# A state-space layer whose batches' closing and opening share one step, on one Trainium2 core

## The chip, the core and the metric

The kernel runs on 1 core of one Trainium2 chip. The metric is device time in microseconds (us) for one execution, lower is better. The engines are named as in the profile: PE is the matmul engine, DVE the vector engine, ACT the scalar (activation) engine, POOL the GpSimd engine, SP the queue that issues transfers.

## What is computed

A decoder of four layers, twelve sublayers in all, on `x` of 4 batches of 1024 tokens, 256 features each, float32. Each sublayer is `x = layernorm(x + sublayer(x))`. The change touches one of the twelve, the state-space layer (`L2_attn`):

```python
def _L2_attn_ref(x, norm_w, in_proj_w, conv_w, conv_b, x_proj_w, dt_proj_w, dt_proj_b, A_log, D, out_proj_w):
    # inner width 512, 16 states, 4 taps, rank 64
    x_copy = x
    h = x * jax.lax.rsqrt(jnp.mean(x * x, axis=-1, keepdims=True) + 1e-05) * norm_w
    xs, res = jnp.split(h @ in_proj_w.T, 2, axis=-1)
    xc = conv_general_dilated(xs over the tokens, conv_w, 4 taps, causal, one filter per feature) + conv_b
    u = silu(xc)
    delta, Bm, Cm = jnp.split(u @ x_proj_w.T, [64, 80], axis=-1)
    delta = softplus(delta @ dt_proj_w.T + dt_proj_b)
    # for every token: state = exp(delta * -exp(A_log)) * state + delta * u * Bm ; y = sum_n state * Cm
    y = y + u * D
    y = y * silu(res)
    return y @ out_proj_w.T + x_copy
```

The layer returns `x_copy` too, so the sum that is normalised behind it is `2 * x + y @ out_proj_w.T`.

## The kernel before

The residual stream stays on the chip for the whole program, as `chip.xt` (128 partitions x 2 feature chunks x 4096 tokens), features on partitions. The program is a row of *steps*. A step is one block in which each engine has its own hand-written instruction list, with semaphores between them; it ends in `all_engine_barrier`, so no engine starts the next step before all have finished this one. The order within an engine is exactly as written; no scheduler moves anything.

`state_space` (L3120) loads the weights and then runs a hardware loop (`nc.Fori`, L3167) over the four batches. `halves` is 2: a batch's 1024 tokens are worked in two groups of 512. `SC` is 4: the inner width of 512 is four chunks of 128. `FC` is 2, the chunks of the 256 features. One turn of the loop is four steps:

- `ssm_inputs` (L3177), the **opening**. ACT squares x (L3197), PE sums the squares over the features with a matmul by constants (L3216), ACT takes the root (L3201), DVE the reciprocal (L3232) and the scaled input `ssm_in` (L3234), for one half and then the other: both halves use the same buffer `rms`, so the second root waits until the first half is scaled. Only when both halves are scaled does PE run the 16 input products (L3223, jobs `(m, j)`: chunk m, half j; 32 matmuls). ACT copies the first eight into `ssm_x` (L3207) and puts the last eight through Silu into `ssm_gate` (L3209).
- `ssm_steps` (L3239). DVE does the convolution, for each of four chunks one multiply-add with a scalar (L3269) and three with an accumulator (L3271), out of `ssm_x` into `ssm_pre`; ACT puts each chunk through Silu into `ssm_u` (L3323); PE multiplies with `x_w` and `states_w` (L3352, L3353) and ACT copies the sums out (L3325). The rest of the step makes the decays' exponents and the rows for the scan.
- `ssm_scan` (L3391), 64 scans of 1024 tokens (16 states x 4 chunks) on DVE, with PE, ACT and POOL around them. Its buffers are `decay`, `state` and `term`. Its last instruction is DVE's multiplication with the gate (L3494).
- `add_norm` (L98), the **closing**. PE multiplies with `out_w` (L138, 16 matmuls), DVE adds twice the residual (L184), ACT squares (L170), PE sums over the features into 4 columns for each half (L151, 1-column matmuls), ACT takes roots (L173), DVE reciprocals (L198), PE spreads them over the partitions (L157), DVE writes the normalised residual (L203).

A float32 matmul is two rows of the trace, called *passes* below: the 32 matmuls of L3223 are 64 rows. Of on-chip matmul memory (8 banks) the closing took all 8, and the opening 6.

## Time and profile before

| what | us |
| --- | --- |
| median of 3 runs | 10751.27 |
| lowest, highest run | 10743.31, 10764.56 |
| the profiled execution, its own time | 10734.41 |
| its span, from the first to the last instruction | 10731.0 |
| the state-space layer's loop in it (four batches) | 5741.61 to 7240.34 |

The profile is of one execution. Lines such as L3223 are lines of the program before. The mean granted clock of PE over the span is 0.855 of full speed (2.4 GHz). The state-space loop is 1499 us of the 10731, some 375 us for each batch; the other eleven sublayers are the rest, and the change leaves them alone.

### The profile page before, as it was taken

The numbers are of one execution on the slowest core, as the hardware profiler recorded it, in microseconds if no ns is written. First come the engines' busy times: TensorE is split into PE (matmuls) and PEld (weight loads), VectorE is DVE, ScalarE is ACT, GpSimd is POOL, SyncE is SP. The second block draws the span as 40 slices with busy tenths as digits, with TensorE's granted clock in tenths as the row PEclk, the third lists the DMA queues.
The fourth block names the chain that finished last, engine by engine and source line by source line (L and its number), as shares of the span: only waits on it lengthen the run. The fifth ranks groups of instructions, "written<-read, shape, count | busy, mean of one in ns | idle before, by whom it ended". The sixth has DMA issues, their size and how long they took to land. (4 is left out here: it accounts for less than half of the span.)

```text
span 10731.0 us, 120768 instructions
## 1 busy us (share of the span) xinstructions
PE 8366.6 (78%) x42322; PEld 4574.4 (43%) x42322; DVE 5866.2 (55%) x11337; ACT 4361.6 (41%) x7541; POOL 2286.8 (21%) x2066
## 2 busy tenths in 40 slices
PE   4877584975989889889896887888886899656565
PEld 1222253542333356546643444444343444345454
DVE  6777341025767556336525786684643656555554
ACT  3666230112555555326413674562221444333332
POOL 1110112021101011001100442350000100366666
PEclk8888676986999889989996988898887999778787
DMA  3221232112212100000000000000001332366656
GB/s 65 44 45 31 47 70 75 63 55 41 34 29 41 24 13 2 9 12 2 10 0 13 1 1 1 1 1 10 5 1 24 50 52 43 107 188 184 186 179 188
DMA packets 243500, 521.79 MB, mean 49 GB/s; under 512 B 55051, under 2 KB 94837, under 8 KB 241431
## 3 DMA queue, kind: packets, MB, share of 16 engines
q1 hardware_dynamic: 154887, 232.49, 10.9%
q0 software_dynamic: 88064, 282.15, 8.8%
q8 instruction: 324, 5.31, 0.2%
q14 instruction: 225, 1.84, 0.1%
HBM read 425.31 MB, written 75.53 MB: 47 GB/s over the span
## 5 line engine op out<-in xcount | busy, mean ns | idle before, releaser
L818 ACT ACTIVATE probs<-scores 128x1024 f32<-128x1024 f32 (+4 forms) x960 | 868.5, 937 | 889.5 <-PE scores L695 634.1
L907 DVE TENSOR_REDUCE row_max<-ring 128x1 f32<-128x512 f32 (+3 forms) x1792 | 1025.8, 627 | 246.3 <-PE ring L669 220.4
L695 PE MATMUL scores<-query_stack,key_stack 99*128 99x512 bf16 (+3 forms) x2816 | 851.2, 394 | 164.6 <-DVE levels L929 77.8
L3568 POOL DMA_INDIRECT r_got<-in_L_ffn_tables,r_pick_now x832 | 814.2, 979 | 329.6 <-issue 244.9
L3693 PE MATMUL r_psum_y<-r_diagonal,r_got 128*128 128x128 f32 x4096 | 582.2, 311 | 363.5 <-ACT r_diagonal L3750 363.5
L715 PE MATMUL outputs<-probs,head_values 128*32 128x512 f32 (+3 forms) x5632 | 780.4, 629 | 101.8 <-ACT probs L815 99.3
L3693 PEld LDWEIGHTS r_psum_y<-r_diagonal,r_got 128*128 128x128 f32 x4096 | 566.0, 225 | 424.7 <-ACT r_diagonal L3750 419.0
L815 ACT ACTIVATE probs<-levels,quant 128x1024 f32<-128x1024 uint8 x512 | 612.7, 1233 | 326.0 <-DVE levels L929 322.4
L929 DVE TENSOR_SCALAR levels<-scores 128x1024 uint8<-128x1024 f32 x512 | 607.6, 1220 | 179.9 <-PE scores L695 145.1
L669 PE MATMUL ring<-key_stack,query_stack 96*128 96x512 bf16 (+3 forms) x1792 | 608.2, 382 | 63.3 <-DMA key_stack<-normed_parts 39.5
L3502 DVE TENSOR_TENSOR_SCAN state<-decay,added 128x1024 f32<-128x1024 f32 x256 | 571.0, 2271 | 32.4 <-ACT decay L3460 32.4
L695 PEld LDWEIGHTS scores<-query_stack,key_stack 99*128 99x128 bf16 x2816 | 257.4, 104 | 689.1 <-DVE levels L929 279.9
L3437 PE MATMUL state_sums<-term,constants 128*128 128x512 f32 x1024 | 497.6, 609 | 42.7 <-POOL term L3468 34.0
L2994 POOL TENSOR_TENSOR norm_squares<-qk,rope 128x256 f32<-128x256 f32 x256 | 180.8, 740 | 1573.2 <-DVE qk L2918 1573.2
L3852 DVE CUSTOM_DVE_ANT_0 r_scratch<-r_got,r_rows_now 128x256 f32<-128x256 f32 x1024 | 374.3, 423 | 73.1 <-DMA r_got<-in_L_ffn_tables,r_pick_now 61.8
L2725 PE MATMUL window_products<-wide_w,shifted 128*128 128x512 f32 x768 | 365.2, 627 | 58.2 <-DVE shifted L2895 49.6
L3456 ACT ACTIVATE added_rows<-ssm_du_rows,ssm_state_in_rows 128x128 f32<-128x128 f32 x1280 | 398.3, 386 | 3.5 <-PEq L63 3.5
L669 PEld LDWEIGHTS ring<-key_stack,query_stack 96*128 96x128 bf16 x1792 | 171.3, 103 | 500.8 <-DVE row_max L907 302.8
L3049 PE MATMUL gated_psum<-norm_sum,gated_w 128*128 128x512 f32 x768 | 346.4, 614 | 6.8 <-DVE norm_sum L3096 6.8
L3460 ACT ACTIVATE decay<-ssm_dt,a_log 128x1024 f32<-128x1024 f32 x256 | 292.5, 1142 | 127.1 <-DVE state L3502 127.0
L3750 ACT ACTIVATE r_diagonal<-constants,r_act 128x128 f32<-128x128 f32 x1024 | 313.1, 388 | 57.9 <-DVE r_act L3857 57.4
L3428 PEld LDWEIGHTS added<-constants,added_rows 128*128 128x128 f32 x2048 | 246.6, 145 | 162.9 <-issue 135.4
(645 smaller groups left out, 15577.2 us busy)
## 6 DMA issues: line engine op xcount, KB each, us to landing
joined_heads<-heads_out SPq DMA_DIRECT2D x512, 32.0 KB, 2.0
expert_w<-in_L_ffn_w SPq DMA_DIRECT2D x16, 1024.0 KB, 10.9
r_got<-in_L_ffn_tables,r_pick_now POOLq DMA_INDIRECT x832, 3.7
quant_parts<-parts SPq DMA_DIRECT2D x48, 256.0 KB, 4.9
query_stack<-quant_parts SPq DMA_DIRECT2D x48, 256.0 KB, 8.5
key_stack<-quant_parts SPq DMA_DIRECT2D x48, 256.0 KB, 8.8
query_stack<-cross_parts SPq DMA_DIRECT2D x48, 256.0 KB, 8.3
normed_parts<-parts SPq DMA_DIRECT2D x48, 256.0 KB, 5.3
```

What stands on the lines that cost most here:

```text
L669: last = nc.tensor.matmul(out[:, 0:cols], lhs, k_stack[0:max_row, h, j * GROUP:j * GROUP + cols], start=True, stop=not edge)
L695: last = nc.tensor.matmul(out[:, off:GROUP], keys, q_stack[0:rows, h, half * GROUP + off:(half + 1) * GROUP], start=True, stop=not edge)
L715: last = nc.tensor.matmul(o_ps[SLOT * i:SLOT * (i + 1), half % out_banks, off:GROUP], vals, probs[0:k_rows, n % 2, i // 2, i % 2, off:GROU ...
L815: nc.scalar.activation(dst, levels[:, e % 2, :, :], ACT.Exp, bias=quant[:, 4:5], scale=scale).then_inc(probs_ready, 1)
L818: nc.scalar.activation(dst, s_ps[0:k_rows, 2 * (e % 2):2 * (e % 2) + 2, off:GROUP], ACT.Exp, scale=scale).then_inc(probs_ready, 1)
L907: nc.vector.reduce_max(row_max[:, i, qt, at:at + 1], src[:, 0:cols], AX.X).then_inc(ring_read, 1)
L929: ts(levels[:, e % 2, :, :], s_ps[:, 2 * (e % 2):2 * (e % 2) + 2, :], 0.0, QMAX, ALU.max, ALU.min).then_inc(scores_read, 1)
L3437: last = nc.tensor.matmul(sum_ps[:, half(j)], chip.c(C_ID), term[:, i % 2, half(j)], start=(n == 0), stop=(n == STATES - 1))
L3456: last = nc.scalar.activation(scaled[:, i % 2, t, :], du_rows[:, t, c, :], ACT.Copy, scale=b_rows[:, t, n:n + 1])
L3502: nc.vector.tensor_tensor_scan(state[:, i % 2, :], decay[:, i % 2, :], added[:, i % 2, :], 0.0, ALU.mult, ALU.add).then_inc(state_ready, 1)
L3568: nc.gpsimd.indirect_dma_start(out=b["got"][:, n, :], out_offset=None, in_=b["tables"], in_offset=bass.IndirectOffsetOnAxis(ap=b[picks][:, ...
L3693: last = nc.tensor.matmul(y_ps[:, c, t * P:(t + 1) * P], row, b["diagonal"][:, k % 2, n, :], start=False, stop=(k == RHEADS * per - 1 and ...
```

## The change

The loop's body is cut at another place. A new step `ssm_between(closing, opening)` holds a batch's closing together with the next batch's opening and its convolution. It is written out once with only the opening (batch 0), stands in the loop for batches 0 to 2 (closing b, opening b + 1), and is written out once more with only the closing (batch 3). What lies between, `ssm_steps` and `ssm_scan`, is in the loop body for three batches and is written out behind the loop for the fourth. Diff, cut:

```diff
-        with nc.Fori(0, BATCH) as b:
-            ssm_inputs(chip, b, w_in, norm_w, xs, gate)
-            ssm_steps(chip, conv, per_feature, w_x, w_states, w_dt, xs, states, u, dt, du_rows, b_rows, pick, kept)
-            ssm_scan(chip, a_log, pick, kept, states, u, dt, du_rows, b_rows, gate, per_feature)
-            with banks(nc, "norm_psum", [P, 8, GROUP], F32) as norm_ps:
-
-                add_norm(chip, [bass.ds(b * SEQ + j * GROUP, GROUP) for j in range(halves)], norm_ps, keeps=2.0, zero_mean=True,
-                         product=(w_out, lambda j, k: u[:, k, j * GROUP:(j + 1) * GROUP]))
...
+        pre = sb("ssm_pre", [P, SC, SEQ])
+
+        def middle():
+            ssm_steps(chip, pre, per_feature, w_x, w_states, w_dt, states, u, dt, du_rows, b_rows, pick, kept)
+            ssm_scan(chip, pre, a_log, pick, kept, states, u, dt, du_rows, b_rows, gate, per_feature)
+
+        between = lambda closing, opening: ssm_between(chip, closing, opening, w_in, norm_w, conv, per_feature, w_out, xs, gate, u, pre)
+        between(None, 0)
+        with nc.Fori(0, BATCH - 1) as b:
+            middle()
+            between(b, b + 1)
+        middle()
+        between(BATCH - 1, None)
...
+        sq_in = ctx.enter_context(sbuf(nc, "ssm_in_squares", [P, halves, FC, GROUP], F32))
+        rms = ctx.enter_context(sbuf(nc, "ssm_in_rms", [P, halves, GROUP], F32))
+        y_ps = ctx.enter_context(banks(nc, "ssm_out_psum", [P, halves, FC, GROUP], F32))
         in_ps = ctx.enter_context(banks(nc, "ssm_in_psum", [P, 4, GROUP], F32))
...
+        mean_ps = lambda j: in_ps[:, 2 + j, :]
+        rstd_ps = lambda g: y_ps[:, g, 0, :]
...
+                if opens:
+                    for j in range(halves):
+                        for c in range(FC):
+                            nc.scalar.activation(sq_in[:, j, c, :], x_in(c, j), ACT.Square).then_inc(in_squared, 1)
+                    for j in range(halves):
+                        act.wait_ge(in_mean, j + 1)
+                        nc.scalar.activation(rms[:, j, :], mean_ps(j), ACT.Sqrt, bias=chip.eps[:, 0:1]).then_inc(rms_ready, 1)
+                squares(0)
+                squares(1)
+                copied(0, 2)
+                deviation(0)
+                copied(2, 3)
+                deviation(1)
+                copied(3, len(jobs))
...
+                output(0, 0)
+                mean(0)
+                output(0, 1)
+                mean(1)
+                output(1, 0)
+                output(1, 1)
+                inputs(0, 2)
+                variance(0)
+                inputs(2, 3)
+                variance(1)
+                inputs(3, 5)
+                spread(0)
+                inputs(5, 6)
+                spread(1)
+                inputs(6, len(jobs))
...
+                add(0, 0)
+                scaled(0)
+                add(0, 1)
+                scaled(1)
+                add(1, 0)
+                add(1, 1)
+                inverse(0)
+                inverse(1)
+                convolve(0)
+                normalise(0)
+                normalise(1)
+                for c in range(1, SC):
+                    convolve(c)
...
@@ -3319,7 +3414,6 @@
             @block.scalar
             def _(act):
                 for c in range(SC):
-                    act.wait_ge(conv_ready, c + 1)
                     nc.scalar.activation(u[:, c, :], pre[:, c, :], ACT.Silu).then_inc(u_ready, 1)
...
-        decay, state, term = (sb(n, [P, 2, SEQ]) for n in ("decay", "state", "term"))
+        decay, state = spare[:, 0:2, :], spare[:, 2:4, :]
+        term = sb("term", [P, 2, SEQ])
```

`spare` is `pre`. In the new step `output` is the product with `out_w`, `mean` the sum of x's squares, `inputs` the input products, `variance` and `spread` the closing's small matmuls, `add`, `inverse` and `normalise` its work on DVE, `scaled` the reciprocal and the two multiplications of the opening. PE waits for `h_ready` half by half (`j + 1`), where it waited for both. ACT's dummy root ahead of the closing (L164) is gone. In both built programs `decay`, `state` and `term` lie at the same bytes of a partition (from 185184, 193376 and 201568), since `ssm_pre` was the first buffer of the step before the scan and gave its place to `decay` and `state` when that step ended.

PE before: the opening, at the head of the loop's body, and the closing, at its end; between the last row and the next batch's first stand a barrier and the loop's branch:

```order
L3211 UNCONDITIONAL_BRANCH
L3216 MATMUL ssm_mean<-norm_squares,constants 128x512 x4
L3223 MATMUL ssm_in_psum<-ssm_in,in_w 128x512 x32
...
L130 UNCONDITIONAL_BRANCH
L138 MATMUL norm_psum<-ssm_u,out_w 128x512 x16
L151 MATMUL norm_psum<-constants,norm_squares 128x1 x16
L157 MATMUL norm_psum<-constants,norm_root 128x128 x8
```

Nothing of the one can run beside the other there.

PE after, the merged step in the loop, from its start:

```order
L3251 MATMUL ssm_out_psum<-ssm_u,out_w 128x512 x4
L3245 MATMUL ssm_in_psum<-ssm_in_squares,constants 128x512 x2
L3251 MATMUL ssm_out_psum<-ssm_u,out_w 128x512 x4
L3245 MATMUL ssm_in_psum<-ssm_in_squares,constants 128x512 x2
L3251 MATMUL ssm_out_psum<-ssm_u,out_w 128x512 x8
L3276 MATMUL ssm_in_psum<-ssm_in,in_w 128x512 x4
L3259 MATMUL ssm_out_psum<-constants,norm_squares 128x1 x8
L3276 MATMUL ssm_in_psum<-ssm_in,in_w 128x512 x2
L3259 MATMUL ssm_out_psum<-constants,norm_squares 128x1 x8
L3276 MATMUL ssm_in_psum<-ssm_in,in_w 128x512 x4
L3266 MATMUL ssm_out_psum<-constants,norm_root 128x128 x4
L3276 MATMUL ssm_in_psum<-ssm_in,in_w 128x512 x2
```

The same 76 matmuls stand in one row now, the opening's sums of squares under the closing's products, and the closing's small matmuls between the first input products; four more of L3266 and twenty of L3276 follow.

DVE after, the middle of the merged step, behind the scaled inputs (before, the convolution L3269 and L3271 stood at the head of the next step, and the residual's L203 at the end of the closing):

```order
L3303 SCALAR_TENSOR_TENSOR norm_sum<-residual,ssm_out_psum 128x512
L3303 ISA
L3303 SCALAR_TENSOR_TENSOR norm_sum<-residual,ssm_out_psum 128x512
L3316 RECIPROCAL norm_root<-norm_root 128x4 x2
L3328 TENSOR_SCALAR ssm_pre<-ssm_x,conv_w,ssm_vectors 128x1024
L3330 SCALAR_TENSOR_TENSOR ssm_pre<-ssm_x,conv_w,ssm_pre 128x1024 x3
L3322 TENSOR_TENSOR residual<-norm_sum,ssm_out_psum 128x512 x4
```

The first chunk's convolution now stands between the closing's reciprocals and its last four instructions; the other three chunks follow behind them, in the same step as PE's input products.

## Rows read from the trace of the kernel before

**Rows 1.** Stretches: us; busy us per engine (instructions); PE's granted clock; DMA share; GB/s.

```profile
core 0: us, PE busy (x) PEld busy (x) DVE busy (x) ACT busy (x) POOL busy (x), PEclk, DMA share, GB/s
5740.54:5814.59 74.05, 55.25 (x104) 18.95 (x104) 27.94 (x23) 21.20 (x30) 0.00 (x0) 0.83 0.00 0
6089.04:6190.03 100.99, 76.49 (x184) 31.23 (x184) 33.53 (x32) 25.73 (x37) 0.00 (x0) 0.84 0.00 1
6190.03:6463.98 273.95, 233.56 (x960) 135.52 (x960) 235.10 (x140) 194.56 (x414) 138.80 (x102) 0.87 0.00 1
6463.98:6565.33 101.35, 77.65 (x184) 31.43 (x184) 33.53 (x32) 25.73 (x37) 0.00 (x0) 0.84 0.00 1
6838.79:6943.88 105.09, 79.89 (x184) 33.99 (x184) 33.61 (x33) 25.72 (x37) 0.00 (x0) 0.79 0.00 1
7216.40:7240.34 23.94, 21.44 (x80) 12.69 (x80) 5.67 (x11) 4.53 (x8) 0.00 (x0) 0.87 0.00 1
```

**Rows 2.** Timeline, batch 0's closing: start us, us, engine, line, idle before and its releaser.

```profile
6087.81 1.23 DVE L3494 TENSOR_TENSOR ssm_u<-ssm_u,ssm_gate 128x1024 f32<-128x1024 f32 x1
...
6090.53 15.75 PE L138 MATMUL norm_psum<-ssm_u,out_w 128*128 128x512 f32 x32 [4.07 <-PEq L63]
...
6096.14 0.69 DVE L184 SCALAR_TENSOR_TENSOR norm_sum<-residual,norm_psum 128x512 f32<-128x512 f32 x1 [7.10 <-PE norm_psum L138]
...
6106.12 3.66 PE L151 MATMUL norm_psum<-constants,norm_squares 128*128 128x1 f32 x32
...
6109.65 2.03 PE L157 MATMUL norm_psum<-constants,norm_root 128*128 128x128 f32 x16
...
6110.82 2.48 DVE L203 TENSOR_TENSOR residual<-norm_sum,norm_psum 128x512 f32 x4 [0.52 <-PE norm_psum L157]
```

**Rows 3.** Timeline, batch 1's opening.

```profile
6116.99 1.28 ACT L3197 ACT_TABLE_LOAD   x1 [6.91 <-issue]
...
6119.49 3.78 PE L3216 MATMUL ssm_mean<-norm_squares,constants 128*128 128x512 f32 x4 [7.81 <-ACT norm_squares L3197]
...
6124.03 3.35 DVE L3232 RECIPROCAL norm_sum<-norm_sum 128x512 f32<-128x512 f32 x1 [10.72 <-ACT norm_sum L3201]
...
6125.08 3.54 PE L3216 MATMUL ssm_mean<-norm_squares,constants 128*128 128x512 f32 x4 [1.81 <-ACT norm_squares L3197]
...
6129.77 3.35 DVE L3232 RECIPROCAL norm_sum<-norm_sum 128x512 f32<-128x512 f32 x1 [0.82 <-ACT norm_sum L3201]
...
6134.73 29.59 PE L3223 MATMUL ssm_in_psum<-ssm_in,in_w 128*128 128x512 f32 x64 [6.11 <-DVE ssm_in L3234]
...
6162.64 0.60 ACT L3209 ACTIVATE ssm_gate<-ssm_in_psum 128x512 f32<-128x512 f32 x1 [1.12 <-PE ssm_in_psum L3223]
...
6164.35 0.60 ACT L3209 ACTIVATE ssm_gate<-ssm_in_psum 128x512 f32<-128x512 f32 x1 [1.12 <-PE ssm_in_psum L3223]
```

**Rows 4.** Timeline, head of the step behind it.

```profile
6165.63 0.81 DVE L3269 TENSOR_SCALAR ssm_pre<-ssm_x,conv_w,ssm_vectors 128x1024 f32<-128x1024 f32 x1 [30.96 <-PEq L63]
6166.48 3.93 DVE L3271 SCALAR_TENSOR_TENSOR ssm_pre<-ssm_x,conv_w,ssm_pre 128x1024 f32<-128x1024 f32 x3
...
6170.44 1.06 ACT L3323 ACTIVATE ssm_u<-ssm_pre 128x1024 f32<-128x1024 f32 x1 [5.49 <-DVE ssm_pre L3271]
...
6171.55 1.97 PE L3352 MATMUL ssm_low_psum<-ssm_u,x_w 128*64 128x512 f32 x2 [7.23 <-ACT ssm_u L3323]
...
6190.03 1.02 ACT L3325 ACTIVATE ssm_low<-ssm_low_psum 64x1024 f32<-64x1024 f32 x1 [4.47 <-PE ssm_states_psum L3353]
```

**Rows 5.** Stretches, small closing matmuls of batches 0 and 2; columns as in Rows 1.

```profile
6106.00:6112.00 6.00, 5.68 (x49) 5.36 (x47) 2.23 (x5) 1.16 (x3) 0.00 (x0) 1.00 0.01 3
6856.00:6866.00 10.00, 8.60 (x50) 8.06 (x48) 3.61 (x7) 1.16 (x3) 0.00 (x0) 0.64 0.01 2
```

**Rows 6.** Timeline, entry into the loop, first batch.

```profile
5739.02 1.52 DVE L237 TENSOR_SCALAR out_w<-out_w,weight_means 128x256 f32<-128x256 f32 x4
5741.61 1.28 ACT L3197 ACT_TABLE_LOAD   x1 [8.97 <-PEq L63]
```

More of the change, by code:

```diff
@@ new lines, in ssm_between @@
+        jobs = [(m, j) for m in range(2 * SC) for j in range(halves)]
+        half = lambda j: slice(j * GROUP, (j + 1) * GROUP)
+        x_in = lambda c, j: chip.xt[:, c, bass.ds(opening * SEQ + j * GROUP, GROUP)]
+        x_out = lambda c, g: chip.xt[:, c, bass.ds(closing * SEQ + g * GROUP, GROUP)]
+        with step(nc, "in_squared in_mean rms_ready h_ready in_ready in_copied y_ready summed squared var_ready root_ready inverse_ready rstd_ready dve_step") as (
+                block, in_squared, in_mean, rms_ready, h_ready, in_ready, in_copied, y_ready, summed, squared, var_ready, root_ready, inverse_ready, rstd_ready, dve_step):
@@ new lines, in squares, with deviation @@
+                def squares(g):
+                    for c in range(FC if closes else 0):
+                        act.wait_ge(summed, FC * g + c + 1)
+                        nc.scalar.activation(sq[:, g, c, :], z[:, g, c, :], ACT.Square).then_inc(squared, 1)
+                def deviation(g):
+                    if closes:
+                        act.wait_ge(var_ready, g + 1)
+                        nc.scalar.activation(root[:, g, :], rstd_ps(g)[:, 0:per], ACT.Sqrt, bias=chip.eps[:, 0:1]).then_inc(root_ready, 1)
@@ new lines, in spread, with inputs @@
+                def spread(g):
+                    if closes:
+                        pe.wait_ge(inverse_ready, g + 1)
+                        for t in range(per):
+                            last = nc.tensor.matmul(rstd_ps(g)[:, t * P:(t + 1) * P], root[:, g, t:t + 1].to_broadcast((P, P)), chip.c(C_ID), start=True, stop=True)
+                        last.then_inc(rstd_ready, 1)
+                def inputs(first, end):
+                    for n in range(first, end if opens else first):
+                        m, j = jobs[n]
+                        pe.wait_ge(h_ready, j + 1)
+                        if n >= 4:
+                            pe.wait_ge(in_copied, n - 3)
+                        for c in range(FC):
+                            last = nc.tensor.matmul(in_ps[:, n % 4, :], w_in[:, c, m * P:(m + 1) * P], h[:, c, half(j)], start=(c == 0), stop=(c == FC - 1))
+                        last.then_inc(in_ready, 1)
@@ L3388, with ssm_scan @@
 TURNED_BY_POOL = 3
[L3391 removed]
+def ssm_scan(chip, spare, a, pick, kept, states, u, dt, du_rows, b_rows, gate, per_feature):
     nc = chip.nc
```

123 lines of the change are left out of this document (62 added, 61 removed).

## The prediction

> **What bounds the kernel now.** I read the page's list of engines and its costliest lines first, then the table of stretches around the state-space layer, then the timeline there. The other eleven sublayers don't change, so only this layer's loop matters. A batch of it falls into a middle and a boundary. The middle (from the copy L3325 to the gate L3494) takes 273.95 us with DVE busy 235 [rows 1]; its instructions are the same before and after, and the scan's buffers lie at the same bytes, so I let it stand. The boundary, from the end of L3494 to the next batch's copy L3325, takes 100.99, 101.35 and 105.09 us at the three places, 307.4 in all. DVE is busy for 33.5 us of each and ACT for 25.7, PE for 76.5, and with its clock at 0.84 [rows 1]. So no engine fills a boundary: it is a chain of steps in which one engine works and the others wait at a barrier.
>
> The pieces of the first boundary, by the timeline: 1.49 us from the gate's end (6087.81 + 1.23) to PE's first product [rows 2]; closing 22.77, to the end of L203 at 6113.30 [rows 2]; 3.69 of barrier and loop branch to ACT's table load at 6116.99 [rows 2, 3]; opening 47.96, to the end of the last Silu at 6164.95 [rows 3]; 0.68 of barrier; 5.92 for the first chunk's convolution and Silu, until PE starts at 6171.55; 18.48 for the products with x_w and states_w, until the copy at 6190.03 [rows 4]. Sum 100.99.
>
> Inside the opening PE stands still while ACT and DVE make the scaled input: from 6119.49, its first mean, to 6134.73 it does 7.3 us of work in 15.2, and the last stretch is two reciprocals of 3.35 us one behind the other [rows 3]. In the closing PE is never idle for more than a handoff, but DVE and ACT are. That is what a merge can use.
>
> **The merged step.** PE's list is what sets its length if nothing in it waits. The closing's 32 passes take 15.75 us, with a slow start in it [rows 2]. The four means, 8 passes, ran at a low clock, 3.78 and 3.54 us [rows 3]; under the products they are in a warm stretch, where four passes take 1.71 us (the distance of the last two Silus, 6162.64 and 6164.35 [rows 3]), so 3.4. The input products are 64 passes, 16 jobs x 1.71 = 27.4 (29.59 before, with a slow start [rows 3]). The small matmuls are 3.66 and 2.03 [rows 2]. Sum 52.3, and 0.6 for the last Silu: 52.9.
>
> Does anything in it wait? I lay the lists against each other, from PE's start as 0. ACT squares x from 0 to 2.3 (two take 1.15, the 1.15 to 1.2 between ACT's table load and PE's first mean [rows 3]), before PE's first mean at 5.5. Roots, reciprocal and scaling take 5.7 us for a half, from PE's mean (6119.49 + 3.78) to 6128.95 [rows 3]; the first half is scaled at 13.0, and the second, with one add before it on DVE, at 18.6. PE gets to the input products at 19.3, so they don't wait, by 0.7 us. Squares of the sums are ready at 20.9, and PE's second small group comes at 26.3. The two small roots come back at 25 and 28.6, their spreads stand at 31.5 and 34.2. DVE is free for the convolution at 28.9. A chunk takes 4.7 us (0.81 + 3.93 [rows 4]), the four residuals 2.5 [rows 2]: 28.9 + 18.8 + 2.5, and half a microsecond for a wait on the second spread, makes 50.7. That is 2.2 us before PE and ACT are done. So the convolution is hidden, with 2.2 us to spare; each microsecond more on DVE beyond that would lengthen the step by one.
>
> Closing and opening together go from 22.77 + 47.96 = 70.73 to 52.9: **17.8** less. One barrier goes, **0.7** [rows 3, 4]. The next step starts with a Silu of 1.06 us instead of 5.92 until PE starts, 1.1 with the handoff: **4.8** less [rows 4]. Behind it the 18.48 stays: PE's 32 passes there are back to back whether the other chunks come early or not (the fourth Silu was ready when PE got to it). One boundary gains 23.3, three gain **69.9**.
>
> **The loop's branch.** The loop turns three times instead of four, and the third boundary has no branch back. A turn costs 3.69 [rows 2, 3]; entering the loop costs 1.07, from the end of L237 (5740.54) to ACT's load [rows 6]. I take the difference, **2.6**, once. What the trace shows is that the way back costs more than the way in. The Trainium skill, "Runtime: NRT & Kernel Launch", section "Instruction fetch mechanics", says why this can be: a taken branch to code that isn't held makes the engine fetch it first, while straight code is streamed ahead. By that rule the copy of the middle behind the loop, which no taken branch back leads to, costs nothing and the sum is the one below; if new code cost as much as a turn, the sum would be 2.6 less.
>
> The copy of the middle is code that the trace of before does not show. Its bounds from rows are nothing and one turn's extra, 2.6. I take nothing, since the first batch entered code that had not run before at 1.07 [rows 6].
>
> **First opening and last closing.** The first stretch takes 74.05 [rows 1]. After, ACT needs no table load in front of its squares (the order has none there; 1.28 [rows 6]), and the second half's means and root don't wait for the first half's scaling. Means start at 1.2, the first half is scaled 9.46 later, the second 4.96 after that [rows 3], at 15.6; then 60 passes at 0.43 (25.8) and a slow start of 1.7, the last Silu: 43.7 against 47.9. That is 4.2, and 4.8 for the convolution, less 0.4 for entering the loop there: **8.6**. The last closing, 23.94 [rows 1], loses its early table load: the roots' load now stands behind the squares, 1.28 at most, mostly under PE's small matmuls. I take **-0.3**; bounds 0 and -1.28.
>
> **Clock.** The third boundary was 4.1 us longer than the first: in its small matmuls the granted clock was 0.64 against 1.00 [rows 5]. I leave one such spell in. It may go (4.1 more gain) or come at all three (8.2 less). PE's start after the merged step comes after 5.4 us of idling (0.6 + 3.7 + 1.1) instead of 7.23, so I leave its slow start in; its price is four passes at 3.78 instead of 1.71, 2.1 [rows 3]. The trace shows a slow start after 4.07 us of idling too [rows 2]. The Trainium skill, "TensorE: Matmul & The Clock Gate", Part 1, says that an array that has idled is granted half the pulses, and all after sustained work; rows 2, 3 and 5 fit that, and by it the merged step, with no idling in it, would keep the high level of 2.4 GHz.
>
> **Sum.** 69.9 + 2.6 + 8.6 - 0.3 = 80.8. The profiled execution took 10734.4 (its span 10731.0), so its like would take 10653.6. The median is 16.9 above it, so I subtract from the median, 10751.3: **10670.5**, 0.75% less.
>
> **Rivals.**
> - *More is gained*: PE stays at the high clock over the shorter gaps in all four steps behind an opening (4 x 2.1) and the slow spell goes (4.1): 10658. For it: the gap is shorter, at the copied middle only some 2.7 us. Against: 4.07 us were enough to go slow. 15%.
> - *The merged step stretches*: PE's waits for h_ready are only 0.7 us clear and DVE's end 2.2; with the slow level in the small matmuls and the products behind them in every boundary, 6 us each, 18 in all: 10689. For it: rows 5. Against: PE has 512-column work on both sides of each small group. 17%.
> - *It doesn't do what it says*, because the moved work was hidden before: about 10748. Against it: DVE waited 30.96 us in front of the convolution [rows 4] and PE 6.11 in front of the products [rows 3]. 4%.
> - *Slower*: PE runs the merged step at the low level, 1.2 GHz, throughout. A pass of 512 columns takes 0.43 at the high level (1.71 / 4 [rows 3]) and twice that at the low one; its 104 passes (32 + 8 + 64) would take 44.7 us more, and from some 63 slow passes in each boundary the 80.8 are gone, at 104 the time is 10671 + 3 x 44.7 = 10805. For it: nothing but that the step mixes tiny matmuls in, and rows 5. Against: the products with out_w and in_w came up to speed after at most some six passes each. 4%.
>
> **How the numbers follow.** Forecast 60%: around 10671, with 8 us of scatter between runs (lowest to median of the three shown) on either side, the spell's 4.1 and 8.2 and the closing's 1. To hold 8 in 10 the range takes in the first two rivals: down to 10658 less 10, up to 10689 plus 11: 10648 to 10700. 0.2%, 21.5 us, is about what a measurement of this kernel can tell from no change. Faster by more: 60 + 15 + 17 = 92%; same 4%; slower 4%.
>
> **What would show it.** The boundary in the loop: 77.7 us instead of 101, of which the merged step is 53 from PE's first product to the last Silu; PE without idle time in it; DVE's last convolution ended 2 us before the last Silu; the next step's first Silu at its very start. The third boundary some 2.6 shorter than the first two. The middle unchanged at 274. It is wrong if PE waits at the first input product, if DVE ends last, if the granted clock in the step is under 0.9, or if the middle after the loop is longer than those in it.

## The result, and the profile after

The changed kernel took 10649.2 us (median of four runs, 10625.6 to 10659.0), the kernel before in the same comparison 10750.3 (four runs, 10743.3 to 10764.6). The ratio is 0.9904, 95% interval 0.9889 to 0.9919: faster by 1.0%, where 0.75% was forecast; 0.9904 of 10751.3 is 10648, at the very edge of the range, 22 us below the forecast. The profiled run took 10658.0, its span 10656.2.

The first view is again the table of stretches: the opening (from the end of L237 to the first L3419, which was L3325 before), the three boundaries (end of the gate, now L3589, to the next L3419) and the last closing. The rows that answer to them are [rows 1]. Columns: stretch, us, busy us per engine (instructions), PE's granted clock, DMA share, GB/s.

```profile
core 0: us, PE busy (x) PEld busy (x) DVE busy (x) ACT busy (x) POOL busy (x), PEclk, DMA share, GB/s
5752.48:5816.42 63.94, 53.65 (x104) 18.57 (x104) 28.12 (x22) 19.58 (x28) 0.00 (x0) 0.88 0.00 0
6091.53:6170.72 79.19, 72.15 (x184) 30.04 (x184) 33.41 (x32) 22.45 (x35) 0.00 (x0) 0.91 0.00 1
6443.25:6519.56 76.31, 69.84 (x184) 29.46 (x184) 33.42 (x33) 22.44 (x34) 0.00 (x0) 0.93 0.00 1
6794.28:6868.06 73.78, 69.86 (x184) 29.45 (x184) 33.41 (x33) 22.44 (x34) 0.00 (x0) 0.95 0.00 1
...
7139.60:7163.40 23.80, 21.39 (x80) 12.66 (x80) 5.68 (x10) 4.33 (x7) 0.00 (x0) 0.87 0.00 1
```

PE has the same 184 passes in a boundary, in 74 to 79 us instead of 101 to 105. It is busy for 91 to 95% of a boundary, where it was for 76%. DVE's 33.4 us are as before, ACT's 22.4 are 3.3 fewer, mostly two table loads of 1.28: the work is the same, the waiting is gone.

The second view is the timeline of the merged step that closes batch 1 and opens batch 2, in order of time (start us, us, engine, line, operation, and in brackets the idle time before it with its releaser; one row can hold several instructions, as x8 says):

```profile
6442.03 1.22 DVE L3589 TENSOR_TENSOR ssm_u<-ssm_u,ssm_gate 128x1024 f32<-128x1024 f32 x1
...
6444.40 5.10 PE L3251 MATMUL ssm_out_psum<-ssm_u,out_w 128*128 128x512 f32 x8 [3.72 <-PEq L63]
...
6449.33 1.88 PE L3245 MATMUL ssm_in_psum<-ssm_in_squares,constants 128*128 128x512 f32 x4
...
6455.48 1.41 DVE L3310 SCALAR_TENSOR_TENSOR ssm_in<-residual,ssm_norm,ssm_in_rms 128x512 f32<-128x512 f32 x2 [0.16 <-DVE ssm_in_rms L3308]
...
6456.20 7.03 PE L3251 MATMUL ssm_out_psum<-ssm_u,out_w 128*128 128x512 f32 x16
...
6460.90 1.42 DVE L3310 SCALAR_TENSOR_TENSOR ssm_in<-residual,ssm_norm,ssm_in_rms 128x512 f32<-128x512 f32 x2
...
6463.07 3.60 PE L3276 MATMUL ssm_in_psum<-ssm_in,in_w 128*128 128x512 f32 x8
...
6466.50 1.84 PE L3259 MATMUL ssm_out_psum<-constants,norm_squares 128*128 128x1 f32 x16
...
6478.72 17.33 PE L3276 MATMUL ssm_in_psum<-ssm_in,in_w 128*128 128x512 f32 x40
```

No row of PE behind the first carries an idle time, through out_w's products, the sums of squares, the input products and the small groups: PE works from 6444.40 on without a wait. The second half of the scaled input is there at 6462.32 (6460.90 + 1.42), 0.75 us before the first input product at 6463.07. That product doesn't need it: its job is of the first half, and PE waits half by half. The first half was scaled at 6456.89 (6455.48 + 1.41), and the first job that needs the second half starts four passes later, at 6464.78. So the waits were clear by 6.2 and 2.5 us.

The end of that step and the head of the next, from the timelines of ACT, DVE and PE:

```profile
6496.10 0.60 ACT L3212 ACTIVATE ssm_gate<-ssm_in_psum 128x512 f32<-128x512 f32 x1 [1.12 <-PE ssm_in_psum L3276]
6500.24 3.89 ACT L3417 ACTIVATE ssm_u<-ssm_pre 128x1024 f32<-128x1024 f32 x4 [3.55 <-issue]
...
6490.60 3.92 DVE L3330 SCALAR_TENSOR_TENSOR ssm_pre<-ssm_x,conv_w,ssm_pre 128x1024 f32<-128x1024 f32 x3
...
6501.35 1.97 PE L3446 MATMUL ssm_low_psum<-ssm_u,x_w 128*64 128x512 f32 x2 [5.29 <-ACT ssm_u L3417]
```

DVE's last convolution ends at 6494.52, 2.18 us before the last Silu's end at 6496.70. Then ACT stands still for 3.55 us while the loop turns, and PE for 5.29. In front of the middle behind the loop the same two rows read:

```profile
6848.98 3.89 ACT L3417 ACTIVATE ssm_u<-ssm_pre 128x1024 f32<-128x1024 f32 x4 [1.02 <-PEq L63]
...
6850.09 1.97 PE L3446 MATMUL ssm_low_psum<-ssm_u,x_w 128*64 128x512 f32 x2 [2.76 <-ACT ssm_u L3417]
```

1.02 us against 3.55: the difference, 2.5, is what the loop's way back costs ACT.

Cut into the pieces of the prediction, in us (from PE's first product to the last Silu's end is the merged step):

| | forecast, in the loop / behind it | boundary 0 | boundary 1 | boundary 2 |
|---|---|---|---|---|
| gate's end to PE's first product | 1.49 | 1.41 | 1.15 | 1.12 |
| merged step | 52.9 | 53.94 | 52.30 | 52.57 |
| last Silu's end to PE's next product | 4.8 / 2.2 | 4.94 | 4.65 | 2.12 |
| until L3419 | 18.48 | 18.90 | 18.21 | 17.97 |
| sum | 77.7 / 75.1 | 79.19 | 76.31 | 73.78 |

The merged step took 53.94 us in boundary 0 and 52.3 to 52.6 in the others. The difference lies at its start, where PE runs out_w's products behind an idle time of 3.7 to 4 us: the granted clock of the first 8 us was 0.61 in boundary 0 and 0.82 in boundary 1. The last closing shows the same in two traces of the changed kernel. It took 23.8 us in this one, with 0.83 over its first 10 us, and 27.0 in the repeat below, with 0.66. The rows are the starts of boundary 0 and 1 and then the closings of this trace and of the repeat:

```profile
6092.94:6100.94 8.00, 8.00 (x12) 3.43 (x13) 0.69 (x1) 3.47 (x5) 0.00 (x0) 0.61 0.00 1
6444.40:6452.40 8.00, 8.00 (x16) 3.58 (x17) 1.12 (x2) 4.16 (x6) 0.00 (x0) 0.82 0.00 0
...
7139.60:7149.60 10.00, 8.95 (x18) 4.09 (x19) 1.03 (x2) 0.63 (x1) 0.00 (x0) 0.83 0.01 2
...
7153.99:7163.99 10.00, 8.91 (x14) 3.85 (x15) 0.69 (x1) 0.63 (x1) 0.00 (x0) 0.66 0.01 2
```

Such a slow start comes and goes between traces of one kernel, and is worth 1.6 us in a merged step and 3.2 in the last closing.

The whole layer, from the end of L237 to the residual's last write, took 1499.8 us before (5740.5 to 7240.3) and 1410.9 after (5752.5 to 7163.4): 88.9 less, of which the boundaries 78.2, the opening 10.1, the last closing 0.1 and the middles 0.5. The spans of the two profiled runs differ by 74.8 only: the layer began 11.9 us later in the run of the changed kernel, behind instructions that are the same in both, and what follows it took 2.2 us longer. The medians differ by 101 us, and the ratio makes it 103. The traced execution of before took 16 us less than its kernel's median, that of after 9 us more, so the two traces can't place the 12 to 14 us that the medians have beyond the layer's 89. The comparison was repeated below for this reason.

### The profile page after: what moved, and what is told of

Its sections match the earlier page's. It is cut to its first block and busy times, and to the rows that moved or that the text cites. A ratio compares the mean times of both kernels' runs of the same rounds, so it can differ in the third digit from the quotient of the medians.

```text
span 10656.2 us, 120727 instructions
## 1 busy us (share of the span) xinstructions
PE 8354.1 (78%) x42322; PEld 4572.8 (43%) x42322; DVE 5866.7 (55%) x11337; ACT 4348.3 (41%) x7530; POOL 2286.5 (21%) x2066
## 5 line engine op out<-in xcount | busy, mean ns | idle before, releaser
L3597 DVE TENSOR_TENSOR_SCAN ssm_pre<-ssm_pre,added 128x1024 f32<-128x1024 f32 x256 | 570.9, 2271 | 32.3 <-ACT ssm_pre L3555 32.3
L3555 ACT ACTIVATE ssm_pre<-ssm_dt,a_log 128x1024 f32<-128x1024 f32 x256 | 292.4, 1142 | 127.0 <-DVE ssm_pre L3597 127.0
```

The costliest lines, as they stand in the source:

```text
L3597: nc.vector.tensor_tensor_scan(state[:, i % 2, :], decay[:, i % 2, :], added[:, i % 2, :], 0.0, ALU.mult, ALU.add).then_inc(state_ready, 1)
```

## Experiments

The theory after the result: all of the gain that the change makes is in the four openings and closings of this layer, by the sum of the prediction with terms mis-sized; what differs from boundary to boundary is the loop's branch and PE's clock at the start of a step. The rivals: that one of the two halves of the change does all of it; that the branch is not what makes the third boundary shorter, or that a straight copy costs as much; that DVE's slack decides; that the extra 14 us of the first comparison are real. The layer's times below are taken from each kernel's trace between the same two instructions, since a layer can be read to some microseconds there, while a comparison of whole runs has an interval of about 20 us.

The kernel before took about 10970 us in all later comparisons, 220 more than in the first, but its layer was the same (1499.8 and 1499.1, below). Ratios, and the layer's microseconds, can be compared over these; times can't. The traces show where the 220 lie: the last sublayer, which fetches rows of tables by POOL's transfers, took 1505.7 and 1504.5 us in the traces of before and after, and 1698.6 to 1731.1 in the eleven later ones. Between 9320 and 10600 us the DMA engines moved 186 GB/s in the trace of before and 161 in that of `before_again`. Why is not shown. The change doesn't touch that sublayer, but its 32 us of spread, and the 42 in what runs ahead of the layer (5740.5 to 5782.6 at its start), stand in every whole-run time.

**The change again**, unchanged, beside the three kernels that follow.

> The changed kernel once more, in five rounds. Theory A (the gain is the state-space layer's alone: from the end of L237 to the end of the residual's last write it took 1499.8 us before and 1410.9 in the first profile after, 88.9 less): the ratio to the kernel before is 0.9917, and the layer takes 1411 within 3 us again. Theory B (the rest of the program gains too, which would make the 101 us between the first medians): ratio at or under 0.9906, with the layer unchanged.

Measured: 0.9931, 0.9908 to 0.9953. Layer 1414.3, boundaries 79.14, 78.88, 73.32. It was 0.9904 the first time; here the gain is nearer to 0.75% than to 1%. Of the 3.4 us by which the layer is longer than in the first trace, 3.2 are the slow start of its last closing, 27.0 us.

**The merge without the convolution.** The step is merged, the convolution stands at the head of the next step, as before:

```diff
                 inverse(1)
-                convolve(0)
                 normalise(0)
                 normalise(1)
-                for c in range(1, SC):
-                    convolve(c)
...
             def _(act):
                 for c in range(SC):
+                    act.wait_ge(conv_ready, c + 1)
                     nc.scalar.activation(u[:, c, :], pre[:, c, :], ACT.Silu).then_inc(u_ready, 1)
```

> The merged step as in the changed kernel, but the convolution stays at the head of the next step, as before the change. Theory A (terms add up: the moved convolution is worth 4.8 us at each of the four places): the layer takes 1411 + 19 = 1430, the step behind the merge needs 5.9 us again until PE starts. Theory C (the merge needs the convolution's work to pay, or hides part of it twice): the layer differs from 1430 by over 5 us. In the merged step PE's stream of 52.3 us stays as it is by both.

Measured: 0.9926, 0.9906 to 0.9946. Layer 1428.7, for 1430 expected, so 71.1 less than before:

```profile
6125.17:6205.92 80.75, 71.04 (x184) 29.87 (x184) 33.34 (x32) 22.78 (x34) 0.00 (x0) 0.92 0.00 1
6478.13:6558.92 80.79, 71.76 (x184) 29.84 (x184) 33.35 (x32) 22.79 (x35) 0.00 (x0) 0.90 0.00 1
6831.95:6912.15 80.20, 71.25 (x184) 29.89 (x184) 33.34 (x32) 22.79 (x34) 0.00 (x0) 0.91 0.00 1
```

The three are nearly equal: the third boundary, behind which the loop doesn't turn, is only 0.6 shorter. The head of the step, in the loop and as the timeline has it:

```profile
6181.78 0.81 DVE L3373 TENSOR_SCALAR ssm_pre<-ssm_x,conv_w,ssm_vectors 128x1024 f32<-128x1024 f32 x1 [17.80 <-PEq L63]
...
6186.59 1.06 ACT L3427 ACTIVATE ssm_u<-ssm_pre 128x1024 f32<-128x1024 f32 x1 [6.13 <-DVE ssm_pre L3375]
```

DVE starts 1.32 us behind the last Silu's end (6180.46), and is the first engine to work there. So with a turn DVE takes 1.3 us to come back, with 0.8 to 1.0 without one here. ACT and PE take longer to come back, but they wait for DVE's first chunk anyway. With the convolution moved ahead, ACT is first, and its 3.55 us lie open. The branch's price is not one number: it depends on which engine has the first work behind it.

**The convolution without the merge.** Opening and closing stay steps of their own; DVE's list of the opening ends with the four chunks:

```diff
                     last.then_inc(h_ready, 1)
+                for c in range(SC):
+                    dve.wait_ge(in_copied, halves * (c + 1))
+                    acc = pre[:, c, :]
+                    then(nc.vector.tensor_scalar(acc, xs[:, c, 0:SEQ], conv[:, c, 0:1], per_feature[:, 0, c:c + 1], ALU.mult, ALU.add))
+                    for k in range(1, TAPS):
+                        then(nc.vector.scalar_tensor_tensor(out=acc, in0=xs[:, c, k:k + SEQ], scalar=conv[:, c, k:k + 1], in1=acc, op0=ALU.mult, op1=ALU.add))
```

> The kernel before with only the convolution moved: it stands at the end of the opening's list on DVE, loop, closing and opening stay apart. Theory A: it is hidden under the input products there too (PE runs 29.6 us of them, DVE needs 19 behind the second copy), so the layer gains 4 x 4.8 = 19 and takes 1481. Theory C (it can only be hidden in the merged step): under 10 us of gain, DVE ending after the last Silu of the gate.

Measured: 0.997, 0.9954 to 0.9986. Layer 1469.3, 30.5 less than before. I look at the head of the first step behind the opening, PE's row first, then the stretch from that row to the copy that ends it, with the same stretch behind boundary 0:

```profile
5824.15 1.07 PE L3345 MATMUL ssm_low_psum<-ssm_u,x_w 128*64 128x512 f32 x2 [2.39 <-ACT ssm_u L3316]
...
5824.15:5840.52 16.37, 16.32 (x32) 3.48 (x32) 0.00 (x0) 2.80 (x4) 0.00 (x0) 1.00 0.00 0
6192.40:6208.86 16.46, 16.32 (x32) 3.48 (x32) 0.00 (x0) 2.89 (x4) 0.00 (x0) 1.00 0.00 0
```

The prediction's term for the moved convolution was 4.8 a batch, 19 in all, and the expectation missed by 12: the kernel gains 30.5. The 4.8 is right at all four places (from the last Silu's end to PE's next product 1.76 instead of 6.60), 19.4 in all. PE came back at the full granted clock in all four heads, 16.37 us instead of 18.46 to 18.97, 9.1 in all. The spell of low clock of [rows 5] isn't there, and the last closing had a slow start of 3.2.

The two halves of the change are not additive: 71.1 + 30.5 = 101.6, together 85.5 (the changed kernel in this comparison). By pieces of the traces the 16.1 are: 8.0 of the full clock in the heads, which the changed kernel doesn't get (its heads took 17.8 to 18.9); 5.1 between the last Silu and PE's next product, where the turn of the loop lies open on ACT only when both are done; 3.5 up to the last Silus, mostly the spell of low clock in the trace of before [rows 5], which either kernel counts as its gain; and 2.7 in the middles, which vary by that much between traces of one kernel. Against that, 3.1 us of a slower last closing are counted twice.

**Without the loop**: four straight copies of the middle.

```diff
         between(None, 0)
-        with nc.Fori(0, BATCH - 1) as b:
+        for b in range(BATCH - 1):
             middle()
             between(b, b + 1)
```

> The changed kernel with the loop over batches written out, so that no branch goes back. Theory A (a turn costs 2.6 us more than an ordinary end of a step, the term of the prediction): the two merged steps that ended in a branch are followed by the next Silu after 1.0 us instead of 3.5, the layer takes 1411 - 5 = 1406. Theory D (the cost is that of reaching code that is not at hand, which straight code pays too when it is new): the gap stays at 3.5 or moves elsewhere, and the layer stays at 1411.

Measured: 0.9933, 0.9912 to 0.9954. Layer 1397.4, for 1406 expected. That is 16.9 less than the changed kernel beside it, of which 3.4 are that one's last closing, and 13.4 less than its first profile, of which 4.9 lie in the middles and 8.4 in the boundaries:

```profile
6082.10:6156.56 74.46, 70.06 (x184) 29.55 (x184) 33.41 (x33) 22.41 (x34) 0.00 (x0) 0.94 0.00 1
6428.08:6501.30 73.22, 69.64 (x184) 29.38 (x184) 33.41 (x32) 22.41 (x35) 0.00 (x0) 0.95 0.00 1
6772.94:6846.12 73.18, 69.53 (x184) 29.36 (x184) 33.41 (x33) 22.42 (x35) 0.00 (x0) 0.95 0.00 0
```

All three boundaries are now nearly as long as the one behind the loop was (73.3 to 73.8), and the middles took 274.2, 271.5, 271.6 and 271.7, where the changed kernel's took 275.1, 272.5, 274.7 and 271.5. So new code that is run straight costs nothing that these rows show. What a turn cost is read behind it: from the last Silu to the copy L3419 the first two boundaries took 22.9 to 23.8 us in three traces of the changed kernel, and 20.3 and 19.8 here. That is 2.8 to 4.0 a turn, 2.4 to 3.1 of it in ACT's wait (0.72 and 1.17 here for 3.52 to 3.88), the rest in PE's slower starts behind the longer pause. What the boundaries differ by beyond that is the start of the merged step in front of the turn. The Trainium skill ("Runtime: NRT & Kernel Launch", section "Instruction fetch mechanics") says that straight code is fetched ahead, and that a taken branch to code that isn't held has to fetch it first; the trace agrees that the turn costs and the straight copy doesn't, but no run shows what the engines do in that time. In the comparison of whole runs the 17 us, 0.15%, don't show: this kernel had 0.9933 and the loop 0.9931, each uncertain by 0.2%.

**The branch at another place.** The loop is rotated, so that the turn lies behind a middle, in front of a merged step:

```diff
         between(None, 0)
+        middle()
         with nc.Fori(0, BATCH - 1) as b:
-            middle()
             between(b, b + 1)
-        middle()
+            middle()
         between(BATCH - 1, None)
```

> The changed kernel with the loop's body turned: opening, middle, then three turns of (merged step, middle), then the closing. The branch back then stands ahead of the merged step, where PE starts first and ACT's first work (squares, 2.2 us) is needed only 5.1 us after PE's start, instead of ahead of a step that begins with ACT's Silu. Theory F (the branch costs ACT 2.6 us, and PE and DVE well under 1, as the version with the convolution left behind the branch shows for DVE, 1.3 against 1.0): the cost is hidden, PE starts within 1.5 us of the gate's end, and the layer takes 1400 to 1405. Theory D (every engine needs some 3.7 us to reach the body's start): the gap moves ahead of PE's first product, 3.7 there, and the layer stays at 1410 to 1414.

Measured: 0.9919, 0.9897 to 0.9941. Layer 1411.3, boundaries 74.30, 79.11, 77.33. The start of merged step 0, with no turn in front of it, then of step 1, with one (its gate ended at 6459.70):

```profile
6115.60 5.53 PE L3251 MATMUL ssm_out_psum<-ssm_u,out_w 128*128 128x512 f32 x8 [4.15 <-PEq L63]
...
6465.06 6.60 PE L3251 MATMUL ssm_out_psum<-ssm_u,out_w 128*128 128x512 f32 x8 [7.93 <-issue]
...
6463.55 2.19 ACT L3227 ACTIVATE ssm_in_squares<-residual 128x512 f32 x4 [15.91 <-issue]
```

PE's first product comes 5.36 and 5.16 us behind the gate where the loop turns, 1.58 and 1.35 where it doesn't (the last is the closing's; 3.5 us of the layer are a slow start there). ACT comes after 3.85 and 3.75, but here PE is first, and PE's time decides. So the expectation that the gap would move ahead of PE's product held (it was 5.2 to 5.4 and not 3.7), and the one by which moving the turn to PE would hide it fell: PE takes longer over a turn than ACT does. The boundaries' sum, 230.7, lies within those of the changed kernel (226.9 to 231.4), and so does the layer (1410.3 to 1414.3).

**DVE's slack**: in each merged step with a convolution, the last chunk's convolution is done a second time, with the same values.

```diff
                 for c in range(1, SC):
                     convolve(c)
+                if closes:
+                    convolve(SC - 1)
```

> The changed kernel with the last chunk's convolution done twice in each of the three merged steps of the loop (four more instructions on DVE, 4.8 us; same values written). Theory A (PE's stream sets the step's length and DVE ends 2.2 us before ACT's last Silu): DVE now ends 4.8 - 2.2 = 2.6 us behind it, each of the three steps is 2.6 longer, the layer 8 us, 1422. Theory E (DVE's end has nothing to do with the step's length, or DVE's work disturbs PE): the layer stays at 1414, or grows by 3 x 4.8 = 14.

Measured: 0.9921, 0.9901 to 0.9941. Layer 1421.1. The first merged step's end:

```profile
6171.64 3.92 DVE L3330 SCALAR_TENSOR_TENSOR ssm_pre<-ssm_x,conv_w,ssm_pre 128x1024 f32<-128x1024 f32 x3
...
6172.33 0.60 ACT L3212 ACTIVATE ssm_gate<-ssm_in_psum 128x512 f32<-128x512 f32 x1 [1.12 <-PE ssm_in_psum L3276]
6179.59 2.00 ACT L3419 ACTIVATE ssm_u<-ssm_pre 128x1024 f32<-128x1024 f32 x2 [6.66 <-issue]
```

DVE gets 4.8 us more and ends 2.63 behind the last Silu (6175.56 and 6172.93), where it ended 2.18 ahead: the slack was 2.2, as reckoned. ACT's pause is 6.66 instead of 3.55, at the three places 3.1, 3.0 and 2.9 more than in the first trace. The boundaries are 82.26, 81.93 and 76.44. Their sum is 9.3 more than that of the first repeat, 11.4 and 13.7 more than those of the other two traces. From the last Silu to PE's next product it is 8.4 to 8.7 against all three, for 8 expected; the rest is PE's level at the start of the merged steps and heads. So the work hid up to the slack, and the 2.6 us beyond it cost about 2.8 to 3.1 at each place.

**The Silu moved too.** If each Silu of the convolution runs between the gate's Silus, the next step starts with PE. Without the loop, and with:

```diff
-                copied(3, len(jobs))
+                copied(3, 9)
+                gated = 9
+                for c in range(SC if opens else 0):
+                    n = (9, 11, 13, 15)[c]
+                    copied(gated, n)
+                    gated = n
+                    act.wait_ge(conv_ready, c + 1)
+                    nc.scalar.activation(u[:, c, :], pre[:, c, :], ACT.Silu)
+                copied(gated, len(jobs))
```

> The version written out without a loop (layer 1397.4), and the four Silus of the next step's u moved into the merged step too, between the gate's Silus on ACT, so that the next step begins with PE. Theory A: ACT has the time (18.5 us busy in 52), and each of the four places saves the 1.1 us from the step's start to PE's: 1397.4 - 4.5 = 1393. Theory G (a Silu that waits for a convolution holds back a copy, and PE waits for its bank): the merged steps are over 53.5 us and the layer is at 1397 or more.

Measured: 0.9898, 0.9878 to 0.9919. Layer 1391.3, for 1393 expected, 6.1 less than without the loop alone, and 9.3 less up to the last closing, which had a slow start here (26.8 us for 23.7). ACT's end of the step, and PE's head behind it with its stretch:

```profile
6166.33 1.05 ACT L3244 ACTIVATE ssm_u<-ssm_pre 128x1024 f32<-128x1024 f32 x1
6167.55 0.60 ACT L3212 ACTIVATE ssm_gate<-ssm_in_psum 128x512 f32<-128x512 f32 x1 [0.18 <-PE ssm_in_psum L3284]
...
6169.01 1.04 PE L3453 MATMUL ssm_low_psum<-ssm_u,x_w 128*64 128x512 f32 x2 [1.50 <-PEq L63]
...
6169.01:6185.34 16.33, 16.29 (x32) 3.45 (x32) 0.00 (x0) 0.00 (x1) 0.00 (x0) 1.00 0.01 2
```

ACT waited 1.12 us in front of nearly every Silu of the gate before, and now 0.18 or nothing behind each moved Silu of 1.05 us: the four found room in these waits. PE starts 0.86 us behind the last Silu's end (6168.15), and with pauses of 1.31 to 1.50 us keeps its full clock: 16.33 in all four heads, where the kernel without the loop took 17.91 to 17.99 with pauses of 2.4 to 2.9. The 9.3 are 6.5 in the heads and 4.7 in the pauses, less 2.0 by which the merged steps were longer (53.69, 53.22 and 52.49, with low clocks at the start of the first two).

**The halves of the opening**, in the kernel before: squares and roots have buffers for each half, and PE waits half by half. Nothing is merged.

```diff
-                pe.wait_ge(h_ready, halves)
                 for n, (m, j) in enumerate(jobs):
+                    pe.wait_ge(h_ready, j + 1)
```

> The kernel before with only the opening's two halves taken apart: own buffers for squares and root per half, all squares first, PE's products waiting half by half. Nothing is merged or moved. Theory A (the opening is a chain through two reciprocals, and the term for the first opening is 4.2 us of which 1.3 is a table load that stays here): 2.9 us for each of four openings, 12 in all, the layer at 1488. Theory H (PE's start at the low clock happens twice, once for the single job of the first half): 1 us or less for each opening, the layer at 1495 or more.

Measured: 0.9989, 0.9978 to 1.0, not told from no change. Layer 1489.8, 10.1 less where 12 were expected, with a slow start of 3.2 in its last closing. The opening took 71.71, 2.3 less than before, the boundaries 97.57, 101.02, 101.47: where nothing else differs, this small part of the change is worth 2 to 3 us a batch by itself. Two of its boundaries show the low clock in the small matmuls again (granted 0.80 over the boundary, 0.85 in the first), of which the second's row is:

```profile
6502.43 4.20 PE L151 MATMUL norm_psum<-constants,norm_squares 128*128 128x1 f32 x32
```

4.20 us, where [rows 2] have 3.66; in the third boundary it is 4.65.

**The three that decide, again**: the kernel before against itself, the changed one, and the one with the Silu moved.

> The kernel before, measured as if it were a changed one: what the comparison says of no change at all. Theory A (the 101 us between the first medians are 86 to 89 us of the state-space layer and scatter of the eleven other sublayers, whose starts differ by up to 12 us between two profiles of the same code): the ratio is 1 within 0.002, with medians up to 15 us apart, and the layer takes 1500 within 5. Theory B (the comparison is exact to a few us, so the 101 has a cause in the program's rest): the two medians agree within 5 us.

> The changed kernel a third time, beside the kernel before and its double on the same chip. Theory A: ratio 0.992 within 0.002, layer 1411 to 1415. Theory B: ratio 0.9906 or lower, as in the first measurement.

> The version without a loop and with the Silus in the merged step, a second time, beside the changed kernel on the same chip: by the layers' times (1391.3 against 1414.3) it is 23 us faster than the changed kernel, ratio to before 0.990. By scatter alone (Theory B's opposite, that the layer's gain is lost in the rest) it would be within 10 us of it.

Measured: before 0.9996 (0.9985 to 1.0008), layer 1499.1; the change 0.9926 (0.9899 to 0.9954), layer 1410.3; with the Silu moved 0.9906 (0.9885 to 0.9927), layer 1394.5, its median 24 us under the changed kernel's, for 23 by the layers. Two medians of one kernel differ by 9.5 us here. The boundaries of the kernel before are 101.02, 104.80, 100.04: this time the spell of low clock is in the second one (its L151 took 4.86 us, the others' 3.66). All three measurements of the change (0.9904, 0.9931, 0.9926) are compatible with one value between 0.9908 and 0.9919, and its layer's gain lies at 85.5 to 88.9 in all three traces (the last against that of `before_again`), 0.8% of the whole.

## Where the prediction was off, and what of it held

**The step that failed is the sum: its terms were mis-sized, and so was the scatter around it.** The terms made 80.8 us, and the layer gained 88.9. The largest error is the spell of low clock: the prediction left one of 4.1 us in the changed kernel, and none came. The scatter was put at 8 us to either side, and the medians took 12 to 14 us more than the layer explains. Where those lie stays open; no run ties them to the change. With the terms at their measured sizes the forecast would have been 10751.3 - 88.9 = 10662: the terms bring it 8 us down, and the scatter did the other 13 to 14.

**The mechanism held.** The merged step is set by PE's list: 52.9 forecast, 52.3 to 53.9 measured, no wait inside. DVE's end was clear by 2.2 us forecast and 2.18 measured, and doubling one chunk showed what lies beyond. The third boundary is shorter by 2.5 to 5.4, forecast 2.6; the upper end has a slow start of the first merged step in it. The middles didn't change (0.5 us in all four).

**One wait was misread.** The prediction laid the second half's scaling against the first input product and found 0.7 us of room; the same distance measured 0.75. But the first product waits for the first half alone. The room was 2.5 us for the second half and 6.2 for the first, so the rival by which the merged step stretches had less to stand on than its price says.

**The spell of low clock.** In the trace of the changed kernel there is none in a merged step, nor in any of the eight other traces that have one: the granted clock there is 0.90 or more over every boundary. The spell came in closings that are steps of their own, at changing places: the third boundary of the first trace [rows 5], the second of the repeat, two in the kernel with halves. That is four in the twelve boundaries of the four traces without a merge, and none in 27 merged steps. The last closing's longer times, in seven of the thirteen traces, lie mostly in its slow start. The 4.1 us by which the third boundary was longer than the first aren't all in its small matmuls: 2.9 lie in the closing, 1.0 in the input products, 0.5 in the head, less 0.3 from the gate to PE. I had a reason in the prediction ("PE has 512-column work on both sides of each small group") and used it only against a rival, not in the sum. No run tests that reason by itself.

**The opening was mis-sized by 1.5**: 10.1 measured, 8.6 forecast. Its last Silu ends 0.7 us earlier than reckoned, PE starts 1.88 behind it for 2.18, since entering the loop costs nearly nothing extra (0.77 us to the first Silu, 0.65 at a plain end) where I had kept 0.4, and its products took 17.96 for 18.48.

**The boundaries without the spell** were 229.3 in sum, forecast 230.5: the merged step as forecast at the mean, the way from the gate to PE 0.3 shorter at each, the stretch until L3419 0.1. The last closing gained 0.1, where I had a loss of 0.3. In all the layer gained 88.9 where 80.8 was forecast: 4.1 for the spell, 1.5 the opening, 1.2 the boundaries, 0.4 the closing, 0.5 the middles (7.7 of the 8.1; the rest is that the second boundary was 0.4 longer before than the first, on which the terms rest).

**The scatter** was taken from three runs of one kernel, lowest to median, 8 us; they agree within 21. The four runs of the changed kernel already lie 33 us apart (10625.6 to 10659.0), the same ratio came out as 0.9904, 0.9931 and 0.9926, and both repeats gave 0.2 to 0.3% less gain than the first measurement. The two profiled runs of the first comparison went the other way by 14 us in identical code. So nothing shows a gain of the change in this part, and the likeliest reading is scatter, by which the first measurement stands at the low edge. With the ratio of either repeat the time would have been 10672 to 10677, beside the forecast of 10670.5; that closeness is luck in its turn, since the layer's terms were 8 us short.

**The rivals.** "More is gained", 10658, held in one of its two parts, the spell. The other part, the full clock in the heads, came only where the pause was shorter or the convolution alone was moved: the changed kernel's heads took 18.90, 18.21 and 17.97, for 18.48 forecast and 16.4 at full clock. "The merged step stretches" fell: the granted clock was 0.94 to 0.97 in it. "It doesn't do what it says" and the low level throughout fell with the table of stretches. On the branch the straight copy was taken at nothing: the third boundary and the unrolled kernel bear it out. What the forecast didn't say is that the turn lies open on whichever engine works first behind it; the 3.7 was ACT's price, and ACT was first before and after.

## What to carry to other kernels

Two steps of a layer in which each engine waits in turn can be joined, and the joined step's length is then the sum of one engine's list; to forecast it, lay the other engines' lists against that one with their clear times, since DVE's 2.2 us held to a tenth of a microsecond; take care which half or chunk each wait is for. A loop's way back is paid by the engine that has the first work behind it, so ask after a merge who is first now. A gain below 1% is better read from the layer's own trace between two fixed instructions than from the whole time, whose ratio moved by 0.3% between repeats; and the scatter of a forecast is taken from the spread of many runs, and not from three.

## What was not expected of the hardware

A turn of the loop costs each engine differently. From the last work in front of it to an engine's first work behind it, it took ACT 3.5 to 4.0 us, PE 5.2 to 5.4 and DVE 1.3; a plain end of a step took 0.65 to 1.6 for ACT, 0.9 to 1.6 for PE, and 0.7 to 1.0 for DVE.

PE's clock after a short pause isn't told by the pause alone. After 2.39 to 2.40 us it came back at the full granted clock in all four heads of the kernel with the moved convolution (16.4 us for the stretch); in the kernel without the loop, after 2.40 to 2.91, it began lower in all four. Rows of both, the second with the stretch from it:

```profile
5789.96 1.57 PE L3446 MATMUL ssm_low_psum<-ssm_u,x_w 128*64 128x512 f32 x2 [2.40 <-ACT ssm_u L3417]
...
6138.58 1.97 PE L3446 MATMUL ssm_low_psum<-ssm_u,x_w 128*64 128x512 f32 x2 [2.91 <-ACT ssm_u L3417]
...
6138.60:6156.56 17.96, 17.92 (x32) 3.71 (x32) 0.00 (x0) 2.77 (x3) 0.00 (x0) 0.91 0.00 1
```

Why is open: the same input products stand in front of the first of these rows as in front of the row at 5824.15 above. With 1.31 to 1.50 us of pause it stayed at the full clock four times in four, in both traces of the kernel with the Silu moved. The Trainium skill, "TensorE: Matmul & The Clock Gate", Part 1, lets the level follow from how busy the array has lately been; these rows neither bear that out nor speak against it, and no run here isolates what decides between these two kernels.

The small one-column matmuls, placed between 512-column ones, had no spell of low clock in any merged step (0.94 to 0.97 over the step), while in a closing of its own the group ran slower at times (4.20 to 4.86 us instead of 3.66).
